# A decoder block on one core: near-zero counts of half of the rows taken as signs on ScalarE, and GpSimd's gate chunks ordered behind VectorE's last gate product

## The reference, cut

```
def _stats(x):
    mean = x.mean(-1, keepdims=True)
    std = jnp.std(x, axis=-1, keepdims=True, ddof=1)
    mn = x.min(-1, keepdims=True)
    mx = x.max(-1, keepdims=True)
    l2 = jnp.linalg.norm(x, axis=-1, keepdims=True)
    sp = (jnp.abs(x) < 1e-06).astype(x.dtype).mean(-1, keepdims=True)
    return jnp.concatenate([mean, std, mn, mx, l2, sp], -1)
...
ri = jnp.concatenate([xf, _stats(xf)], -1)
h = jax.nn.gelu(ri @ r1_w.T + r1_b, approximate=False)
probs = jax.nn.softmax(h @ r2_w.T, -1)
```

## Time and profile before

| | us |
|---|---|
| median of 3 runs | 1672.55 (1671.28 to 1672.86) |
| the profiled execution, its own time | 1673.45 |
| its span in the trace | 1671.3 |
| VectorE busy | 943.2 (56%) |
| TensorE busy | 1475.5 (88%) |
| ScalarE busy | 488.6 (29%) |

### The profile page before, as it was taken

One profiled execution on the slowest core, in us unless ns is written; L12 is line 12 of the kernel. 1 busy time (PEld: TensorE's weight loads), 2 busy tenths in 40 slices (PEclk: granted clock), 3 DMA queues, 4 the chain that ended last, 5 costly groups with the idle time before them and its releaser, 6 DMA issues.

```text
span 1671.3 us, 29354 instructions
## 1 busy us (share of the span) xinstructions
PE 1475.5 (88%) x10911; PEld 1127.6 (67%) x10911; DVE 943.2 (56%) x2784; ACT 488.6 (29%) x1154; POOL 310.7 (19%) x400
## 2 busy tenths in 40 slices
PE   5679998998899720699999999999999999999995
PEld 3356555555556410588878888788887878878783
DVE  8667999999996989533333423324233242332454
ACT  4556566675755443010101001010010100101023
POOL 4001121121111200111212121121211212112135
PEclk9689999999999855699999999999999999999997
DMA  6203213132130261067677676776767777676796
GB/s 175 71 22 100 76 64 106 43 99 70 67 86 1 101 280 59 17 220 295 228 286 269 235 291 214 297 258 248 288 217 292 251 260 283 220 294 239 274 349 198
DMA packets 92575, 311.03 MB, mean 186 GB/s; under 512 B 42838, under 2 KB 46940, under 8 KB 83164
## 3 DMA queue, kind: packets, MB, share of 16 engines
q1 hardware_dynamic: 79260, 287.87, 47.1%
q0 software_dynamic: 13248, 22.29, 5.9%
HBM read 273.18 MB, written 36.96 MB: 186 GB/s over the span
## 4 chain that ended last, share of the span: by engine, by line
PE 69%; DVE 20%; issue 5%; ACT 3%; DMA 2%; POOL 1%; SPq 1%; DVEq 0%; POOLq 0%; ACTq 0%
PE bank L1029 36%; PE banks L1043 14%; PE bank L654 6%; PE banks L1046 4%; DVE arena L1447 3%; DVE arena L1437 2%; DVE arena L1886 2%; PE bank L656 1%; PE banks L756 1%; DMA arena<-acc_rows 1%; DVE arena L1619 1%; DVE arena L1609 1%; PE banks L737 1%; DVE arena L1487 1%; DVE arena L1468 1%
## 5 line engine op out<-in xcount | busy, mean ns | idle before, releaser
L1382 ACT ACTIVATE arena<-bank 128x160 f32<-128x160 f32 x288 | 87.1, 303 | 873.2 <-PE bank L1029 871.9
L1029 PE MATMUL bank<-keep,arena 128*128 128x160 f32 x2304 | 320.0, 299 | 1.7 <-DVE arena L2082 1.7
L1029 PE MATMUL bank<-arena 128*128 128x160 f32 x2304 | 319.2, 301 | 0.8 <-issue 0.8
L1029 PEld LDWEIGHTS bank<-keep,arena 128*128 128x128 f32 x2304 | 315.4, 189 | 5.5 <-issue 3.2
L1029 PEld LDWEIGHTS bank<-arena 128*128 128x128 f32 x2304 | 315.4, 191 | 4.2 <-issue 4.2
L2082 DVE TENSOR_TENSOR arena<-arena,bank 128x160 f32<-128x160 f32 x256 | 82.1, 321 | 404.6 <-ACT arena L1382 352.5
L1043 PE MATMUL banks<-arena 128*128 128x512 f32 x576 | 252.4, 592 | 0.0
L2271 POOL DMA_INDIRECT acc_rows<-arena,keep x64 | 102.8, 1606 | 628.8 <-DVE arena L2027 610.9
L1043 PEld LDWEIGHTS banks<-arena 128*128 128x128 f32 x576 | 107.6, 190 | 122.5 <-issue 122.5
L2025 DVE TENSOR_SCALAR arena<-banks,keep 128x512 f32<-128x512 f32 x32 | 24.0, 750 | 189.3 <-PE banks L1046 185.6
L654 PE MATMUL bank<-arena 128*128 128x512 f32 x224 | 108.0, 627 | 7.1 <-DVE arena L1447 7.1
(11 more groups left out here) (294 smaller groups left out, 1803.7 us busy)
## 6 DMA issues: line engine op xcount, KB each, us to landing
arena<-in_wup SPq DMA_DIRECT2D x32, 4096.0 KB, 12.5
arena<-in_wdn SPq DMA_DIRECT2D x32, 2048.0 KB
arena<-in_aup SPq DMA_DIRECT2D x32, 512.0 KB, 11.6
arena<-in_xT SPq DMA_DIRECT2D x32, 256.0 KB, 2.8
arena<-in_kT SPq DMA_DIRECT2D x8, 1024.0 KB, 5.6
arena<-in_v SPq DMA_DIRECT2D x32, 256.0 KB, 6.6
x_rows<-arena SPq DMA_DIRECT2D x8, 1024.0 KB, 4.5
acc_rows<-arena SPq DMA_DIRECT2D x8, 1024.0 KB, 6.8
```

The source lines that it names most:

```text
L1029: m = pe.matmul(u[:, g * CAP:(g + 1) * CAP], w, xeT[e.slot][:, c, :], start=(c == 0), stop=(c == C - 1))
L1382: act.activation(sg[k], Ub[k][:, 0:CAP], ACT.Silu).then_inc(up_a(f"silu{j}"), 1)
```

## The change

A new ScalarE function, `signs_of_squares(b)`, takes row tiles 0 to `signed(b) - 1` of the squares and writes over them the sign of a difference from the threshold, with the sum of each row as accumulator. The count follows from the sum s of signs as s/2D + 1/2. `signed(b)` is 2 in batches 0 to 5 and 4 in batches 6 and 7. VectorE counts the other tiles as before, which are two in batches 0 to 5 and none in batches 6 and 7. Column 5 of `st6` is scaled in two instructions, the second of which waits for the signs. GpSimd's gate chunks wait for `neg` in place of `max`. The indices of the two best experts are cast straight into their table, which drops one copy of 128x8 per batch on VectorE.

```
+            def signs_of_squares(b):
+                act.wait_ge(*n3_a.at("squares", b))
+                for tb in range(signed(b)):
+                    rows = square_rows(b, tb)
+                    m = act.activation(rows, rows, ACT.Sign, scale=-SPARSE_SCALE, bias=sparse_at,
+                                       accum_out=sums(b)[2][:, tb:tb + 1])
+                m.then_inc(n3_s("sq"), 1)
...
+        def signed(b):
+            return TB if b.off >= NB - 2 else TB // 2
...  in last_values on ScalarE
                 squares(p)
                 norm3_out(b)
+                signs_of_squares(p)
                 last_copies(b)
                 squares(b)
+                signs_of_squares(b)
                 router_stats(p)
...  in step on ScalarE
                 if a:
                     gates_0(n)
+                if r:
+                    signs_of_squares(n - 2)
+                if a:
                     gates_1(n)
...  in router_sparse on VectorE
-                for tb in range(TB):
+                for tb in range(signed(b), TB):
...  in router_stats on VectorE
                 dve.wait_ge(*ro_v.at("cnt", b))
-                dve.tensor_scalar(st6[:, :, 5], nz, 1.0 / D, None, ALU.mult).then_inc(ro_v("stats"), 1)
+                k = signed(b)
+                if k < TB:
+                    dve.tensor_scalar(st6[:, k:, 5], nz[:, k:], 1.0 / D, None, ALU.mult)
+                dve.wait_ge(*n3_s.at("sq", b))
+                dve.tensor_scalar(st6[:, 0:k, 5], nz[:, 0:k], 0.5 / D, 0.5, ALU.mult, ALU.add).then_inc(ro_v("stats"), 1)
...  in top_two on VectorE
+                ex2 = tiles_of(e_all, b)
                 dve.tensor_copy(ex2, at8[:, :, 0:2])
...
-                dve.tensor_copy(tiles_of(e_all, b), ex2)
...  in gate_chunks on GpSimd
-                pool.wait_ge(*ga_v.at("max", b))
+                pool.wait_ge(*ga_v.at("neg", b))
```

More of the change, by code:

```diff
@@ L50 @@
 SPARSE_SQ = 9.99999996004197e-13
+SPARSE_SCALE = 217.0 * 2.0 ** 28
+SPARSE_AT = 0.058250490576028824
 R_AT = TB * GROW
@@ L278, in decoder_kernel @@
         at8 = room.take(TB, 8, dt=U32)
-        ex2 = room.take(TB, 2)
         oh0 = room.take(TB, NE)
@@ L282, in decoder_kernel @@
         wsum = room.take(TB)
+        sparse_at = room.take(1)
         more_w = ST[0].rearrange("p (k c) t -> p k (c t)", k=2)
@@ L365, in decoder_kernel @@
         l2_p = steps("ln2_pool", ["eps2", "rstd2", "eps3", "minus3", "rstd3", "shift3"])
-        n3_a = steps("ln3_scalar", [f"out{tb}" for tb in range(TB)] + ["sq"])
+        n3_a = steps("ln3_scalar", [f"out{tb}" for tb in range(TB)] + ["squares"])
+        n3_s = steps("signs_scalar", ["sq"])
         ro_t = steps("router_tensor", [f"x{tb}" for tb in range(TB)] + ["st", "h0", "h1", "lg"])
@@ L1109, in squares @@
                                        accum_out=sums(b)[1][:, tb:tb + 1])
-                m.then_inc(n3_a("sq"), 1)
+                m.then_inc(n3_a("squares"), 1)
+            def signs_of_squares(b):
[5 more added lines that the diff above has]
+                m.then_inc(n3_s("sq"), 1)
             def queries(b, tiles):
@@ L1414, in _ @@
             dve.memset(posh, 0.5)
+            dve.memset(sparse_at, SPARSE_AT)
             dve.memset(ones, 1.0).then_inc(cs_v("misc"), 1)
@@ L1511, in head_out @@
                     dve.wait_ge(*ro_t.at(f"x{TB - 1}", b - 2))
-                    dve.wait_ge(*n3_a.at("sq", b - 2))
+                    dve.wait_ge(*n3_s.at("sq", b - 2))
                     dve.wait_ge(*ro_v.at("extr1", b - 2))
@@ L1603, in router_sparse @@
             def router_sparse(b):
-                dve.wait_ge(*n3_a.at("sq", b))
+                dve.wait_ge(*n3_a.at("squares", b))
                 dve.wait_ge(*ro_v.at("stats", b - 1))
-                for tb in range(TB):
+                for tb in range(signed(b), TB):
                     rows = square_rows(b, tb)
@@ L1610, in router_sparse @@
                                           accum_out=sums(b)[2][:, tb:tb + 1])
-                m.then_inc(ro_v("cnt"), 1)
+                if signed(b) < TB:
+                    m.then_inc(ro_v("cnt"), 1)
+                else:
+                    dve.sem_inc(ro_v("cnt"), 1)
             def router_extreme(b, k):
```

## The result

The changed kernel takes 1709.42 us (median of 4 runs, 1708.82 to 1709.75). The kernel before, on the same chip, took 1672.7 us (1671.28 to 1673.84). The ratio is 1.022, with a 95% interval of 1.0202 to 1.0237: the change costs 36.7 us. The forecast was 1710 us, in a range of 1703 to 1717.

What follows compares the result with a forecast made beforehand. VectorE was taken to bound steps 2 to 6, TensorE the rest of step 7. Waits 29.25, step 7 4.35 and the end 4.15, less 1.0 for GpSimd's chunks, add 36.75 us: 1710 us, range 1703 to 1717.

Steps and rivals of the forecast that it cites:

- The bound: Steps 2 to 6: VectorE sets the length; work taken from it shortens a step, a wait put in lengthens it.
- The wait: Steps 2 to 6: VectorE idles 7.0 us for ScalarE's signs, the scan starts 5.85 us later; 29.25 us in all.
- the sign: ScalarE: one 128x512 sign taken at 0.61 us from start to start, like the square of the same shape.
- The clock in the steps: Steps 2 to 6: a 1.7 us loss to TensorE's low clock makes it 5.6 us late, still inside VectorE's 5.85.
- Step 7: Step 7, TensorE the path: scores 2.65 us later plus 1.7 us for the clock, 4.35 us.
- The end: End of the pipeline: four signs of batch p delay the copies 2.45 us, plus 1.7 us of clock, 4.15 us.
- GpSimd's chunks: Collision with VectorE over SBUF moves: 1.0 us gained in steps 0 and 1, nothing taken in steps 2 to 6.
- The sum: Whole kernel: 29.25 + 4.35 + 4.15 - 1.0 = 36.75 us added, forecast 1710 us.
- Signs in time: Rival: signs end before VectorE needs them, leaving only the gain, at most 8.3 us, so 1665 us; 2%.
- The clock and the chunks are kinder: Rival: the clock need not fall and every step gains on L1585, 5.35 us less, 1704.9 us; 18%.
- TensorE becomes the bound: Rival: clock stays low longer after the waits, TensorE 7.3 us late a step; 1721 us, or 1713 to 1718; 12%.
- A table load: Rival: ScalarE loads a table before every group of signs, 1.28 us each, 9.0 us in all, 1719 us; 3%.

Runs made afterwards that it cites:

- late_scale: The changed kernel with, in the steps, VectorE's scaling that waits for the signs moved behind the weighing of head pair 3; 1666.90 us, ratio 0.9972.
- no_wait: The changed kernel with the scaling of signed tiles reading row sums, so it waits for no sign (near-zero share wrong); 1666.06 us, ratio 0.9967.
- last_only: The changed kernel with signs in the last two batches alone, four tiles each; batches 0 to 5 counted on VectorE; 1674.79 us, ratio 1.0015.
- pool_only: The kernel before with one edit: GpSimd's gate chunks wait for the last gate product, not the maximum; 1671.71 us, ratio 0.9995.
- late_steps2: The changed kernel with the waiting scaling moved behind head pair 3's weighing, two tiles signed in batches 0 to 5, none in the last two; 1663.12 us.
- late_steps3: The changed kernel with the waiting scaling moved behind head pair 3's weighing, three tiles signed in batches 0 to 5, none in the last two; 1661.26 us.
- signs_early: The changed kernel with the steps' signs moved up ScalarE to directly behind their squares, scaling left ahead of the scan; 1680.95 us, ratio 1.0057.
- four_signs: The changed kernel with all four row tiles signed in every batch, signs and waiting scaling left in place; 1717.06 us, ratio 1.0273.
- end_behind: last_only with the four signs of batch p behind the copies of the last rows instead of ahead; 1675.06 us, ratio 1.002.
- signs_mid: The changed kernel with the steps' signs two places up ScalarE, ahead of the last head's decays and the gates copy; 1701.05 us, ratio 1.0175.

## Why the prediction was right, point by point

**The bound.** VectorE bounds steps 2 to 6. late_scale and no_wait show it from the other side: work taken from it there shortens the step as long as nothing waits.

**The wait, 5 x 5.85 = 29.25 us.** Measured 30.05. The steps that opened at high clock in both kernels are 65.99 us before and 71.98 after, so the wait costs 5.99 us a step; the low openings add about the same in both, 3.3 and 3.4 us. The mechanism, the place and the three numbers of it (7.0 us of idle time, scores 3.9 us late, step still VectorE's) stood. What was off is one term, the sign: 0.71 us from start to start, where I took the square's 0.61 from the earlier trace rows. It is 0.1 us too little from one sign to the next, and 0.4 us too little on four at the end. In a step the scaling starts 2.07 us behind the start of the copy (457.68 to 459.75), where I had 1.92: the first sign came sooner behind the copy than I took (0.48 us, not 0.60), the signs and what follows them took longer. Signs and squares of the same shape differ by that amount too, 0.71 against 0.62 us at the end of the pipeline. The Trainium skill (ScalarE: Activation LUTs, "What ACT_TABLE_LOAD costs") states that an operand that is a pointer to one value per partition adds about 93 ns to an activation. The sign's bias is one (`sparse_at`), the square has none, and the difference of 0.09 us agrees with it; but no run here changed that operand alone, and the two are also different functions.

**The clock in the steps.** I said that a low opening of a step (5.40 us for eight products, not 3.70) stays inside VectorE's lateness. That was wrong, in both kernels alike, and so it cancelled. VectorE, before, at the norm statistics that wait for the retention, ahead of the gates copies of steps 4 and 5, whose openings took 5.40 and 3.70 us:

```profile
288.79 0.69 DVE L1454 BATCH_NORM_STATS2 arena<-arena 128x6 f32<-128x512 f32 x1 [1.97 <-ACT arena L1081]
...
354.78 0.69 DVE L1454 BATCH_NORM_STATS2 arena<-arena 128x6 f32<-128x512 f32 x1 [0.90 <-ACT arena L1081]
```

The wait is 0.9 us after a high opening and 2.0 after a low one, so a low opening costs a step about 1.1 us, as the lengths of the steps have it too (67.05 and 65.99 us). The profiled execution of before had three such steps of five.

**Step 7, 4.35 us.** The gates copy to the selection stage is 102.82 us after and 98.37 in last_only, which has the same end and no signs in step 7: 4.45 us. Right in both parts, the scores 2.95 us late (2.65 and two signs at 0.1 more each, with 0.1 over) and 1.45 us of clock (from the scores to L808 it is 3.53 us, against 2.08).

**The end, 4.15 us.** last_only against before: 98.37 - 95.65 = 2.72 us. The two terms were near (2.66 us of waiting where I had 2.45, by the price of the sign, and 1.7 of clock), and then 1.6 us came back, which I had not foreseen. The second layer of the last batch, before and after:

```profile
586.01 3.68 PE L842 MATMUL banks<-arena 128*128 128x512 f32 x4 [0.68 <-ACT arena L1232]
```

```profile
623.54 1.98 PE L848 MATMUL banks<-arena 128*128 128x512 f32 x4 [0.68 <-ACT arena L1246]
```

Before, these four products ran at the low clock, after at the high one. The four kernels without signs at the end (before, pool_only, late_steps2, late_steps3) ran them in 3.36 to 3.68 us. Of the eight with them, six took 1.98 us (the change, late_scale, last_only, signs_early, four_signs, end_behind), but no_wait took 3.56 and signs_mid 3.60. So the signs go with the high clock here without settling it, and what sets it stays open.

**GpSimd's chunks, -1.0 us and nothing in steps 2 to 6.** Right, by pool_only: -1.0 and +0.13.

**The sum.** The terms missed by +0.8 (steps), +0.1 (step 7), -1.4 (end), +0.2 (steps 0 and 1) and, together, -0.2 for the start and the experts: 36.75 - 0.55 = 36.2. The forecast was nearer than its terms by luck, because the sign's price and the clock's return cancel.

**The rivals.** *Signs in time* would have needed a gates copy seven microseconds earlier, and it didn't move. Where I put them in time (signs_early), the kernel was slower than before. *The clock and the chunks are kinder* described the end in its size and not in its mechanism. *TensorE becomes the bound* did not happen at the change's place. *A table load* did not come: both traces have 28.

## What to carry to other kernels

Work moved to an idle engine is worth what the bound engine saves, less what it then waits for the result; look at when the idle engine comes to it in its written order, and not at how idle it is. Here the same signs brought 5 us or cost 37 us, depending only on where one instruction of 0.17 us waited for them. When a result is taken from another engine, put the instruction that waits for it behind all that others need from this engine, and as late as its own reader allows. And if the move is tried at the source instead, by making the result earlier, ask whom that makes later.

## What the runs showed of the hardware

TensorE's clock at the opening of a step was not settled by the wait ahead of it. In late_scale all five openings have 1.89 us of idle time in their rows, released by VectorE's tap, and 3.70 us for the products; in the kernel before, an opening with the same 1.89 us took 5.40 us in two steps. TensorE, opening a step at 263.86 before and at 324.53 in late_scale:

```profile
263.86 5.40 PE L654 MATMUL bank<-arena 128*128 128x512 f32 x8 [1.89 <-DVE arena L1447]
```

```profile
324.53 3.70 PE L660 MATMUL bank<-arena 128*128 128x512 f32 x8 [1.89 <-DVE arena L1467]
```

The four kernels that took counts off VectorE in the steps and did not make it wait for the signs had a high opening at 5 (late_scale), 5 (no_wait), 4 (late_steps2) and 5 (late_steps3) of five. Before, pool_only, last_only and end_behind had 2, signs_mid and signs_early 1, and the change 1 and a second that was low in part (4.59 us). But four_signs, with the longest waits of all, had 5 of 5, so the waits do not settle it, and what does isn't shown. It matters for the sizes: at 1.1 us an opening, the clock gave late_scale about 3 us in its profiled execution, on top of the 5.8 us that the two counts are worth.
